# Feed-forward down projection ordered by block of hidden values, for four token tiles at once

## What the kernel must compute

```python
xn = _layernorm(x)
s = attention(xn, wq, wk, wv, wo)            # 16 heads, causal, rotary
h = silu(xn @ wg.T) * (xn @ wu.T)            # 256 -> 768
g = silu(h @ wd.T)                           # 768 -> 256, the down projection
out = x + s * g
```

## Time and profile before

| | us |
|---|---|
| median of 3 runs | 1267.53 |
| the profiled execution, its time | 1268.76 |
| its span, from the first to the last instruction | 1267.0 |
| TensorE busy | 1200.6 (95%) |
| VectorE busy | 1011.8 (80%) |
| ScalarE busy | 853.1 (67%) |
| GpSimd busy | 602.7 (48%) |
| granted TensorE clock, mean | 0.986 |

### The profile page before, as it was taken

How to read it: one execution, slowest core, us unless ns; L and a number is a source line. 1 busy time by engine, 2 the same in 40 slices (tenths; PEclk the granted TensorE clock), 3 DMA queues, 4 the chain that set the end, 5 groups by cost and what they waited for, 6 DMA issues and landing times.

```text
span 1267.0 us, 30431 instructions
## 1 busy us (share of the span) xinstructions
PE 1200.6 (95%) x10743; PEld 555.6 (44%) x10743; DVE 1011.8 (80%) x1229; ACT 853.1 (67%) x1074; POOL 602.7 (48%) x934
## 2 busy tenths in 40 slices
PE   4999999999999789999999999999999999999997
PEld 3555555555554423333343344334433433343333
DVE  5665666666667789999999999999999999999943
ACT  3455545545543357778887788788878888888784
POOL 4666566556654313224543454445345434543454
PEclk8999999999999979999999999999999999999999
DMA  6345355454447312313333243143133332431222
GB/s 240 118 139 177 123 159 159 139 157 138 168 130 178 116 28 68 93 43 84 76 96 94 59 120 93 44 116 107 48 94 85 94 93 66 112 94 44 69 69 84
DMA packets 152228, 133.48 MB, mean 105 GB/s; under 512 B 44720, under 2 KB 137392, under 8 KB 151984
## 3 DMA queue, kind: packets, MB, share of 16 engines
q1 hardware_dynamic: 152112, 131.90, 35.8%
HBM read 72.61 MB, written 50.33 MB: 97 GB/s over the span
## 4 chain that ended last, share of the span: by engine, by line
PE 54%; issue 6%; DVE 2%; ACT 2%; DMA 1%; SPq 1%; POOL 0%; DVEq 0%; ACTq 0%; POOLq 0%
PE ps L1333 20%; PE ps L1316 12%; PE ps L773 11%; PE ps L1369 4%; PE ps L781 3%; PE ps L1353 2%; PE ps L1361 2%; DVE mxp L797 1%; ACT pr L1245 1%; DMA qs<-mp 1%; PE ps L1340 1%; SPq L986 1%; ACT ot L1252 0%; POOL mp L1045 0%; DVE yt L1181 0%
## 5 line engine op out<-in xcount | busy, mean ns | idle before, releaser
L797 DVE TENSOR_REDUCE mxp<-ps 128x2 f32<-128x1024 f32 (+2 forms) x576 | 683.5, 1222 | 62.9 <-PE ps L773 33.9
L1245 ACT ACTIVATE pr<-ps 128x1024 f32<-128x1024 f32 x576 | 570.0, 1033 | 168.3 <-PE ps L1316 160.4
L1333 PE MATMUL ps<-pr,vt 128*32 128x512 f32 (+3 forms) x3072 | 314.7, 497 | 1.4 <-ACT ot L1252 0.9
L1055 POOL TENSOR_SCALAR_AFFINE_SELECT pr<-pr 128x256 f32<-128x256 f32 (+1 forms) x448 | 192.2, 449 | 123.3 <-ACT pr L1245 122.0
L1316 PE MATMUL ps<-qs,ks 50*128 50x512 f16 (+3 forms) x1536 | 226.7, 330 | 13.9 <-DMA qs<-mp 3.8
L773 PE MATMUL ps<-ks,qs 48*128 48x512 f16 (+2 forms) x1792 | 227.1, 306 | 8.4 <-DVE mxp L797 4.0
L1045 POOL TENSOR_SCALAR mp<-mneg 32x128 f16<-32x128 f32 x32 | 9.2, 288 | 318.6 <-issue 304.0
L1316 PEld LDWEIGHTS ps<-qs,ks 50*128 50x128 f16 x1536 | 64.8, 93 | 212.7 <-issue 204.6
L662 PE MATMUL ps<-xTh,wguT 128*128 128x512 f16 x384 | 145.8, 380 | 1.5 <-ACT vs L571 1.2
L662 PE MATMUL ps<-xTl,wguT 128*128 128x512 f16 x384 | 145.8, 380 | 0.0
L773 PEld LDWEIGHTS ps<-ks,qs 48*128 48x128 f16 x1792 | 81.9, 94 | 136.6 <-issue 117.3
(11 more groups left out here) (107 smaller groups left out, 1346.4 us busy)
## 6 DMA issues: line engine op xcount, KB each, us to landing
v_d<-vs SPq DMA_DIRECT2D x16, 1024.0 KB, 4.9
vt<-v_d SPq DMA_DIRECT2D x32, 512.0 KB, 4.1
xs<-in_L_attn_x SPq DMA_DIRECT2D x16, 512.0 KB, 4.8
q_parts_d<-parts SPq DMA_DIRECT2D x16, 512.0 KB, 2.9
k_parts_d<-parts SPq DMA_DIRECT2D x16, 512.0 KB, 2.9
gate_d<-gs SPq DMA_DIRECT2D x16, 512.0 KB, 3.3
qs<-q_parts_d SPq DMA_DIRECT2D x64, 128.0 KB, 3.2
ks<-k_parts_d SPq DMA_DIRECT2D x64, 128.0 KB, 3.2
```

Of the source, the lines that this page charges most:

```text
L797: dve.tensor_reduce(dst, ps[:, slot:slot + 2, :].rearrange("p t (n s) -> p (t n) s", s=w), axis=AX.X, op=ALU.max).then_inc(keep["max_dve"] ...
L1055: pool.affine_select(out=blk, in_=blk, compare_op=ALU.is_ge, fill=0.0, base=0, pattern=[[0, 2], [0, len(hs)], [1, P]], channel_multiplier= ...
L1245: act.activation(probs(step, s).rearrange("p (t j) s -> p t j s", t=2)[:, :, hs[0]:hs[-1] + 1, 0:w], ps[:, slot:slot + 2, 0:w * len(hs)].r ...
L1333: ins = pe.matmul(ps[VW * j:VW * (j + 1), O0, lo - c * CH:CH], vt[g % 2][:, kb, j, :], probs(step, s)[:, j, at:at + w], start=first, stop= ...
```

## The change

The loops of the down projection are turned round. The block m is now the outer step and the four token tiles the inner one, and high and low halves are mixed: high 0 to 4, low 0 and 1, high 5, low 2 and 3, low 4 and 5. The 48 matmuls are the same, with the same operands and sums, and so are the 12 waits, now one ahead of every four matmuls. The first signal down_pe (bank V0 complete) now comes two matmuls ahead of the second, where there were twelve between them. The places for work ahead in the last batch stand behind 20, 40 and 48 matmuls instead of 24, 36 and 48.

```diff
-                    for a in (0, 2):
-                        down(a, hh, range(MH - 1))
-                    for a in (0, 2):
-                        down(a, hh, (MH - 1,))
-                    for a in (1, 3):
-                        down(a, hh, range(MH))
+                    def down(part, m):
+
+                        if part is hh:
+                            pe.wait_ge(hid_hi.sem, hid_hi.after(step, m + 1))
+                        else:
+                            wait_low(pe, step, m)
+                        for a in range(CT):
+                            ins = pe.matmul(ps[:, V0 + a // 2, (a % 2) * D:(a % 2 + 1) * D], part[:, m, a * P:(a + 1) * P],
                                             wdT[:, m, :], start=part is hh and m == 0 and a % 2 == 0,
                                             stop=part is hl and m == MH - 1, skip_group_check=True)
+                            if part is hl and m == MH - 1 and a % 2 == 1:
+                                ins.then_inc(down_pe.sem, 1)
+
+                    for m in range(MH - 1):
+                        down(hh, m)
                     peek(step, "down0")
-                    for a in range(CT):
-                        ins = down(a, hl, range(MH))
-                        if a % 2 == 1:
-                            ins.then_inc(down_pe.sem, 1)
-                        peek(step, f"down{a + 1}")
+                    down(hl, 0)
+                    down(hl, 1)
+                    down(hh, MH - 1)
+                    down(hl, 2)
+                    down(hl, 3)
+                    peek(step, "down2")
+                    for m in range(LOW_POOL, MH):
+                        down(hl, m)
+                    peek(step, "down4")
```

More of the change, by code:

```diff
@@ L678, in down @@
                                             stop=part is hl and m == MH - 1, skip_group_check=True)
-                        return ins
-                    for a in (0, 2):
-                        down(a, hh, range(MH - 1))
-                    for a in (0, 2):
-                        down(a, hh, (MH - 1,))
-                    for a in (1, 3):
-                        down(a, hh, range(MH))
-                    peek(step, "down0")
-                    for a in range(CT):
-                        ins = down(a, hl, range(MH))
-                        if a % 2 == 1:
-                            ins.then_inc(down_pe.sem, 1)
-                        peek(step, f"down{a + 1}")
+                            if part is hl and m == MH - 1 and a % 2 == 1:
+                                ins.then_inc(down_pe.sem, 1)
+                    for m in range(MH - 1):
+                        down(hh, m)
+                    peek(step, "down0")
+                    down(hl, 0)
[7 more added lines that the diff above has]
+                    peek(step, "down4")
                 over_batches(pe, chunk)
```

## The result

| | before | after |
|---|---|---|
| median, us (4 runs each) | 1267.82 | 1252.83 |
| lowest and highest | 1267.53, 1269.28 | 1251.68, 1254.95 |
| profiled execution: its time, span | 1268.76, 1267.0 | 1253.75, 1252.0 |

The ratio is 0.9881, with a 95% interval of 0.9864 to 0.9899: 15 us faster, where 17.5 were forecast. The time lies within the range given, 2.8 us above the forecast and also above the 1248 to 1252 us that were called the likeliest case.

The account below looks back on a forecast made before the run. TensorE's program order was taken to bound the first stage. 14 loop chunks at 1.15 (16.1) + 0.88 + 0.88 - 0.35 = 17.5 us gained, giving a median of 1250.0 us, range 1247.5 to 1256.

Parts of the forecast that it names:

- the likeliest case: Whole kernel: 1248 to 1252 us, with the squeeze, the last batch and the clock each allowed to vary; chance 0.72.
- The bound and the size of the waits: First stage: TensorE's order sets the time; two waits in the down projection, 0.93 and 0.22 us, 1.15 a chunk, vanish.
- No cost for changing the output: Down projection: changing output range from matmul to matmul costs 0, within bounds of 0 and 0.16 us each.
- Rival 3: Down projection: the clock falls to the lower level, +3.2 us a chunk, +51 us, 1318 us; chance 0.01.
- The next chunk's slack: Next chunk: GpSimd's rotation starts 0.48 us late, hidden by 1.12 us of slack at the first hidden block; cost 0.
- The last batch: Its two chunks: attention products break the stream, TensorE waits for VectorE's maximum before down4; gain 0.88 us each, not 1.15.
- The squeeze of maxima between hidden blocks: Last batch's first chunk: VectorE's maxima come too late for TensorE's next product; 0.35 us lost, bounds 0 and 0.7.
- The attention has the same instructions and starts that much earlier: Attention: unchanged in length, so the first stage's 17.5 us carry to the span, 1267.0 to 1249.5 us.
- the low clock at its start: Attention's start: the low-clock stretch may begin and end at other moments, moving the end by at most 1 us.
- rival 1: Chunks: only the visible 0.77 us closes (1255.2 us), or up to 0.48 us is handed back (1256.7 us); chance 0.20.

Follow-up runs that it names:

- high_only: Kernel before with only its high halves turned round, blocks outermost and four token tiles inside, low halves still tile by tile; median 1251.71 us, ratio 0.9862.
- high_pairs: Kernel before with high blocks 0 to 3 for all four tiles, then blocks 4 and 5 tile by tile; median 1255.81 us, ratio 0.9897.
- banks: Changed kernel with token tiles taken as 0, 2, 1, 3, so the PSUM bank changes at every matmul; median 1251.31 us.
- less4: Changed kernel without low block 4, 4 of the 48 down projection matmuls left out, output lacks that term; one run, 1246.39 us.
- less20: Changed kernel without low blocks 0 to 4, 20 of the 48 down projection matmuls left out, output lacks those terms; one run, 1239.82 us.

## Why the prediction was right, and where it was short

**The bound and the size of the waits: right.** 1.15 us of waiting a chunk was forecast from distances between matmuls; 1.16 was measured, and high_only and high_pairs took 5.30 and 5.63 us where the same working gave 5.30 and 5.63.

**No cost for changing the output: right**, by banks, at the bound taken (0 of 0 to 0.16 us). Rival 3, the clock that falls with the banks, had a chance of 0.01; the clock of the loop is 1.00 with the bank changed at every second matmul and at every one.

**The next chunk's slack: right.** Forecast 0.48 us late at the rotation, measured 5.67 - 5.22 = 0.45, and hidden; less4 shows 0.44 us of room behind it, less20 that it has an end. The copy of the values (vs), needed one block earlier than the first hidden block, was overlooked in that chain.

**The last batch: right in kind, small misses in size.** 0.88 us for each chunk was 0.94 and 0.95 (the wait before down4 is there, 0.43 us). The squeeze of maxima between hidden blocks was put at 0.35 us and was 1.16 - 1.02 = 0.14, of which 0.13 are seen at the product itself. With 16 x 1.15 less these, 17.5 became 17.97.

**"The attention has the same instructions and starts that much earlier": the step that failed.** It does start earlier, but it took 4.0 us longer in the profiled pair. The prediction had the low clock at its start as a term of at most 1 us. Its end alone moved the first group by 1.5 to 1.8 us against the kernel before, and groups 3 to 5 had no term at all: longer waits of TensorE for the queries, and spells of the low clock behind the longest of them, made a group up to 2.5 us longer, up to three groups in a run. By the means over all runs, 883.2 against 880.9 us outside the first stage, it is 2.3 us. That "the same instructions" take the same time was taken over from before without a row. That the result lies in the range is luck: it was stretched for rival 1, which was not what happened, for no chunk of the loop gave anything back. The spread of the runs would have been a better reason: the kernel before had runs from 1266.9 to 1271.4 us over all comparisons, and the changed one from 1250.5 to 1258.9.

## What to carry to other kernels

Where one engine's order is the time, measure its waits by the distance between starts and the weight loads, not by the idle column: a pipelined row covered 0.16 us of each gap here, so that 0.77 us seen was 1.15 us real. Let the consumer go through the blocks in the order in which they are made, with all independent uses of a block together; here four uses a block, and the high halves alone, gave nearly everything. A gain in one stage is best read from that stage's marks. Then look at the rest of the span in many runs: here stages whose instructions were untouched gave back 2.3 us of 18, and single runs of one kernel lay 8 us apart.

## What the runs showed of the hardware that was not expected

The granted clock fell for single spells of 3.4 us in the middle of busy groups of the attention, in some executions and not in others of one kernel (one, two or three of them in its four profiles). What TensorE did before was the same each time: it had stood idle for 1.61 to 1.78 us and was busy again when the clock fell, 0.1 to 1.7 us later. The group was 2.2 to 2.5 us longer, wait and spell together. At the stage's start the low level lasted 20.5 to 27.3 us, and what came after about 21 us cost 1.5 to 1.8 us; keeping the clock high for the first 16 us, with fillers, gained 0.7 us in the first group.
